# Turning the experts' fetched rows as 16-bit halves instead of 4-byte numbers

## The reference, cut to what matters

```python
x = x + L0_gnn(layernorm(x), ...)      # three graph layers, 50000 edges
x = x + L0_ffn(layernorm(x), ...)      # 8 experts,  256 -> 512 -> 256, gelu
x = x + L1_gnn(layernorm(x), ...)      # graph sum and a GRU cell
x = x + L1_ffn(layernorm(x), ...)      # 16 experts, 256 -> 512 -> 256, relu

# inside a mixture, for every expert e
h   = act(x @ W1[e] + b1[e])           # 512 numbers for each row
y_e = h @ W2[e] + b2[e]                # 256 numbers for each row
y   = y + weight_of_e * y_e            # only where e is one of the row's two best
```

## Time and profile before

| | |
|---|---|
| runs of the kernel before, median (lowest to highest) | 1776.88 us (1776.11 to 1778.33) |
| the profiled execution, its own time | 1773.84 us |
| its span in the trace | 1772.1 us |
| mean granted clock of TensorE | 0.891 of full speed |
| busy: PE, DVE, ACT, POOL | 1473.6, 871.9, 481.6, 336.9 us |
| loops of the first mixture, about | 826 to 1033 us |
| loops of the second mixture, about | 1453 to 1696 us |

### The profile page before, as it was taken

How to read it: one execution, slowest core, us unless ns; L and a number is a source line. 1 busy time by engine, 2 the same in 40 slices (tenths; PEclk the granted TensorE clock), 3 DMA queues, 4 the chain that set the end, 5 groups by cost and what they waited for, 6 DMA issues and landing times. The chain is left out here.

```text
span 1772.1 us, 34488 instructions
## 1 busy us (share of the span) xinstructions
PE 1473.6 (83%) x8498; PEld 1031.8 (58%) x8499; DVE 871.9 (49%) x2496; ACT 481.6 (27%) x1231; POOL 336.9 (19%) x391
## 2 busy tenths in 40 slices
PE   4795989989998999975999956998998649999920
PEld 3674744457443855534898932444665638899820
DVE  6996833323222357774222248312888452222258
ACT  2564400012000311112444433001222414444421
POOL 3000210012000300002554420000000514555420
PEclk9555999999999999986999979998999559999965
DMA  4000321123111422222223257202221334332444
GB/s 122 0 0 12 107 75 47 47 75 119 51 50 47 127 91 83 83 76 85 92 95 127 100 155 234 90 24 74 69 67 42 107 134 155 115 115 92 132 129 129
DMA packets 134622, 158.41 MB, mean 89 GB/s; under 512 B 16929, under 2 KB 119698, under 8 KB 134258
## 3 DMA queue, kind: packets, MB, share of 16 engines
q1 hardware_dynamic: 122642, 125.59, 22.4%
q0 software_dynamic: 11840, 32.12, 6.0%
q10 hardware_dynamic: 96, 0.20, 0.0%
HBM read 103.12 MB, written 57.93 MB: 91 GB/s over the span
## 5 line engine op out<-in xcount | busy, mean ns | idle before, releaser
L875 PE MATMUL agg_ps<-parts,counts 128*128 128x512 f16 x1875 | 410.5, 380 | 8.7 <-PEq L653 8.0
L875 PEld LDWEIGHTS agg_ps<-parts,counts 128*128 (+1 forms) x1875 | 183.6, 98 | 227.6 <-issue 13.5
L1441 ACT ACTIVATE experts_hT<-experts_ps_h,experts_b_col 128x128 f32<-128x128 f32 x456 | 165.8, 367 | 186.4 <-PE experts_ps_h L1416 161.1
L1424 PE MATMUL experts_ps_y<-experts_rows,experts_hT 128*128 128x256 f32 x688 | 163.0, 380 | 0.0
L1379 POOL DMA_INDIRECT chosen<-experts_y,experts_row x116 | 114.6, 988 | 146.6 <-issue 107.9
L1368 POOL DMA_INDIRECT experts_fetched<-tokens,experts_index x120 | 116.1, 967 | 93.9 <-ACT experts_x L1445 41.0
L777 POOL TENSOR_TENSOR parts<-proj_rest,gru_rows 128x256 f32 (+2 forms) x75 | 54.4, 726 | 416.8 <-DVE proj_rest L755 416.8
L1424 PEld LDWEIGHTS experts_ps_y<-experts_rows,experts_hT 128*128 128x128 f32 x688 | 124.3, 191 | 13.4
L1416 PE MATMUL experts_ps_h<-experts_xT,experts_rows 128*128 128x128 f32 x976 | 122.1, 279 | 8.9 <-issue 7.8
L1416 PEld LDWEIGHTS experts_ps_h<-experts_xT,experts_rows 128*128 128x128 f32 x976 | 118.9, 194 | 17.5 <-issue 13.8
L1465 DVE COPY experts_xT<-experts_ps_x 128x256 f32<-128x256 f32 x114 | 48.4, 425 | 162.4 <-PE experts_ps_x L1405 162.4
(11 more groups left out here) (314 smaller groups left out, 2039.5 us busy)
## 6 DMA issues: line engine op xcount, KB each, us to landing
experts_rows<-in_L_ffn_w SPq DMA_DIRECT2D x32, 512.0 KB, 4.8
gru_rows<-x SPq DMA_DIRECT2D x75, 128.0 KB, 2.2
own<-proj_own SPq DMA_DIRECT2D x75, 128.0 KB, 1.7
gru_rows<-own SPq DMA_DIRECT2D x75, 128.0 KB, 2.1
h<-agg_out SPq DMA_DIRECT2D x50, 128.0 KB, 1.7
gru_rows<-h SPq DMA_DIRECT2D x50, 128.0 KB, 2.0
gru_rows<-chosen SPq DMA_DIRECT2D x50, 128.0 KB, 2.3
combine_y<-chosen SPq DMA_DIRECT2D x50, 128.0 KB, 2.1
```

Source lines behind the costliest of these rows:

```text
L875: last = nc.tensor.matmul(ps[b][:], cst.counts[:, s, bass.ds(t * P, P)], parts[:, s, :], start=s == 0, stop=s == NT - 1)
L1424: last = nc.tensor.matmul(ps_y[:, 0:D], hT[:, c, :], down[b][:, c, :], start=c == 0, stop=c == KH - 1)
L1441: nc.scalar.activation(hT[:, c, :], ps_h[c][:, 0:P], function, bias=b1_col[:, bass.ds(e * KH + c, 1)]).then_inc(hT_ready, 1)
```

## The change

The program gets a second identity matrix in 16-bit numbers (`ident16`), which POOL converts from the first in `build_counts`. In `turn`, the tile of 4-byte numbers is viewed as 16-bit numbers, and its lower and its upper halves are turned apart: per half of 128 columns two transposes of 128 by 128 16-bit numbers, four per tile instead of two. The view steps over every second 16-bit number, so the stationary operand is read with a step of 4 bytes. `ps_x` holds 16-bit numbers now, 512 per partition instead of 256. DVE's copy (the new helper `join`) reads them in order and writes each half back beside the other, with a step of 4 bytes, so that `xT` holds 4-byte numbers again. Nothing else in the loop is changed.

```diff
@@ build_counts, GpSimd
                 nc.gpsimd.memset(far_at[:, 0:1], 0.0)
+                nc.gpsimd.tensor_copy(cst.ident16[:], cst.ident[:])
@@ run_experts
-        ps_x, ps_y, ps_b = pb("ps_x", [P, KD, P]), pb("ps_y", [P, BANK]), pb("ps_b", [P, BANK])
+        ps_x = ctx.enter_context(nc.psum_tensor(tag + "ps_x", [P, KD, 2, P], F16))
+        ps_y, ps_b = pb("ps_y", [P, BANK]), pb("ps_b", [P, BANK])
@@ TensorE
                 def turn(q):
                     pe.wait_ge(x_ready, q + 1)
+                    half = x[:].bitcast(F16).rearrange("p (c n h) -> p c h n", c=KD, h=2)
                     for c in range(KD):
-                        last = nc.tensor.transpose(ps_x[:, c, :], x[:, c * P:(c + 1) * P], cst.ident[:])
+                        for h in range(2):
+                            last = nc.tensor.transpose(ps_x[:, c, h, :], half[:, c, h, :], cst.ident16[:])
                     last.then_inc(x_turned, 1)
@@ VectorE
+                def join(ready):
+                    nc.vector.tensor_copy(xT[:].rearrange("p c n -> p (c n)").bitcast(U16).rearrange("p (c n h) -> p c h n", c=KD, h=2),
+                                          ps_x[:].bitcast(U16)).then_inc(ready, 1)
@@ VectorE, before the loop and in it
-                nc.vector.tensor_copy(xT[:], ps_x[:]).then_inc(xT_ready, 1)
+                join(xT_ready)
@@ four_blocks
+        cst.ident16 = sb("ident16", [P, P], F16)
```

More of the change, by code:

```diff
@@ L18 @@
 F16 = mybir.dt.float16
+U16 = mybir.dt.uint16
 I32 = mybir.dt.int32
```

## The result

The change makes the kernel slightly slower: 1782.84 us in the median of 20 runs (1779.36 to 1786.21), against 1779.03 us for the kernel before in 20 runs on the same chips (1774.9 to 1780.62). The ratio is 1.0025, with a 95% interval from 1.0019 to 1.0031, so +4.4 us (3.4 to 5.5). The profiled execution of the change took 1780.89 us, with a span of 1779.1 us. The forecast was 1781.2 us, +4.3, from a before of 1776.88 us.

A forecast was written before the change was run, and what follows sets the result against it. PE's issue was taken to bound both mixture loops. Turns with edges (+0.033 us x 114 = +3.8) and first-tile copies (+0.5) gave +4.3 us on 1776.88, so 1781.2 us, range 1776 to 1809.

The forecast's parts named there:

- The bound: Both mixture loops: time is what PE issues, 3.74 us per tile, 114 tiles.
- The price of four turns: Turn on PE: four 16-bit turns cost 0.223 us per tile where two 4-byte turns cost 0.22.
- The choice of 55.7 ns against 114: One 16-bit turn on PE: strided load stays under the 55.7 ns stream; line 517's strided pair took 114 ns.
- Rival B: Turns on PE: load and stream run one after another, 83.4 ns per turn, 1793.8 us in all; chance 0.15.
- The 27.7 ns: Contiguous 16-bit load of 128 columns on PE, from 25 loads with one-column multiplications; lower bound of one turn.
- The edge: PE passing into 16-bit work and back, once per tile: 0.03 us for both, between 0 and 0.08.
- The prediction's own signs: Turn, period and copy times to check; period growing beyond the turn means unnamed cost, in-loop xT waits a wrong DVE part.
- A: The forecast case: four turns cost what two did, edges aside; 1777 to 1786 us, period 3.74 to 3.78; chance 0.50.
- The copy: DVE's copy to xT grows by 0.27 to 0.69 us, hidden in the loop by PE's second multiplication; price 0.
- The 0.5 us before the two first tiles: Before each mixture's first tile nothing hides the longer DVE copy: 2 x 0.27 = +0.5 us.
- The identity on POOL: One 128 x 128 conversion on POOL, 0.2 to 1 us, ahead of a 125.9 us wait for PE; price 0.
- The sum: Whole kernel: +3.8 us of turns and edges plus +0.5 us of first-tile copies, +4.3 us.

The follow-up runs named there:

- load_step8: The change with the turns' stationary operand read with a step of 8 bytes instead of 4; one execution 1784.63 us against 1775.95 before, tile 3.79 us.
- stream_step8: The change with the 16-bit identity, the moving operand, read with a step of 8 bytes; one execution 1801.83 us against 1775.95 before, tile 3.97 us.
- extra256: The change plus one unused 16-bit multiplication of 256 columns behind the four turns; one execution 1787.51 us against 1773.42 before, median tile period 3.85 us.
- spread_turns: The change with its four turns apart, one at each pair of 4-byte multiplications of the first matrix; one execution 1806.64 us against 1775.95 before, tile 3.95 us.
- copy_alone: The kernel before, its two 4-byte turns kept, with only DVE's copy made as long as in the change (512 2-byte elements); ratio to before 0.9999.
- change_again: The unaltered change timed once more, on one chip; ratio to the kernel before 1.0027, +4.8 us (3.0 to 6.4).
- turns_again: The change with a 256-element copy of upper halves only, no joining, timed again on one chip; ratio to before 1.0016, +2.8 us (0.7 to 5.2).
- turns_alone: The change with a 256-element copy of upper halves only, no joining, first timing, 5 runs; ratio to before 1.0035, +6.2 us (3.9 to 8.5).

## Why the prediction was right, point by point

**The bound.** PE's issue was the bound in both loops, and stayed it: what a tile's work on PE grew by, its period grew by, and 0.3 us more on DVE cost nothing, one tile apart.

**The price of four turns.** 0.223 us was worked out from a 512-column stream, and 0.22 to 0.23 measured. This was the term said to decide, and it was right. The choice of 55.7 ns against 114 for a strided load was right, and load_step8 and stream_step8 show the reason: a step slows the stream and not the load. What the Trainium skill says on this point ("TensorE: Matmul & The Clock Gate", section "Weight-path perf modes — Fast Weight Load (FWL) and DoubleRow"), that the fast load works on strided operands too, the runs bear out as far as a pace can: with steps of 4 and of 8 bytes a turn stays at 56 ns.

**Rival B** falls: loads and streams of short 16-bit pairs overlap. The rule of the Trainium skill of about 81 ns for a pair with 128 columns ("TensorE: Matmul & The Clock Gate", section "Back-to-back issue gap") does not hold here; the four pairs measured 56 ns each. The 27.7 ns that the prediction takes for a bare load was read at 9.23 us, ahead of the first record of the clock in the trace (37.2 us), so the clock it stands for is not known, and no run measured a bare load in the loops.

**The edge.** This is the term that was mis-sized, and its name was wrong. I took 0.03 us, between 0 and 0.08, for going over between types, there and back. Going over to the turns costs nothing: the first multiplication still takes 1.78 us and the four turns 0.22. Coming back costs 0.05 to 0.06 us, and it is no cost of the types: it is the part of the next 4-byte load that a 16-bit turn doesn't cover, 56 ns in the first instruction behind the turns. extra256 makes it vanish with the types unchanged, and spread_turns multiplies it by four. A row of before bounded it: 4-byte multiplications of 128 columns run at 0.112 us, so their loads need no more than that, and at most 0.056 us of one can stay open behind a stream of 0.056. The prediction's own signs showed the miss: the turn came out as A has it, but the period of 3.79 us lies above A's 3.74 to 3.78 and grew by more than the turn, which was to show a cost not named. The Trainium skill ("TensorE: Matmul & The Clock Gate", section "LDWEIGHTS (loading the stationary operand)") gives columns divided by 1.2 for a load in ns, by which an estimate for 128 columns is 107 ns; 107 - 56 = 51 is near the 53 to 56 ns that are left open.

**The copy** was put at 0.69 us and took 0.734; copy_alone shows no price of it in the loop. In the profiled execution of the change it did come on the path once, which was to be a sign that the part on DVE is wrong:

```profile
1683.30 0.39 PE L1410 MATMUL experts_ps_x<-ident,experts_x 128*128 128x128 f16 x4
...
1685.01 0.73 DVE L1458 COPY experts_xT<-experts_ps_x 128x512 uint16<-128x512 uint16 x1 [1.93 <-PE experts_ps_x L1410]
...
1685.79 2.05 PE L1421 MATMUL experts_ps_h<-experts_xT,experts_rows 128*128 128x128 f32 x16 [0.32 <-DVE experts_xT L1458]
```

The copy began 1.71 us after the turns, where it begins 0.43 us after them elsewhere, and 425 ns would have ended 0.31 us sooner. change_again has the same wait in the same tile (0.34 us), while in turns_again, whose short copy begins as late in that tile (1.69 us), PE's multiplications don't wait. So beside late turns the longer copy cost 0.3 us once, and not 0. Why the copy begins late is open.

The 0.5 us before the two first tiles was wrong. From the first turn to the first multiplication it was 1.74 us before:

```profile
824.54 0.69 PE L1405 MATMUL experts_ps_x<-ident,experts_x 128*128 128x128 f32 x2 [3.70 <-DVE experts_x L1455]
...
826.28 3.37 PE L1416 MATMUL experts_ps_h<-experts_xT,gru_rows 128*128 128x128 f32 x16 [1.05 <-DVE experts_xT L1457]
```

and it is 1.74 us after:

```profile
823.86 0.61 PE L1410 MATMUL experts_ps_x<-ident,experts_x 128*128 128x128 f16 x4 [3.85 <-DVE experts_x L1464]
...
825.60 3.78 PE L1421 MATMUL experts_ps_h<-experts_xT,gru_rows 128*128 128x128 f32 x16 [1.13 <-DVE experts_xT L1458]
```

The wait was put down to DVE, but PE started 0.59 us after the copy's end before (825.69) and 0.36 us after it now (825.24); something else ended last, which I take to be PE's own reading of the loop bounds (argued, not tested). The 1.74 us do not change either in extra256, where one more multiplication stands on PE there (826.14 to 827.88). A releaser that is long done when the waiter starts is the sign to look for.

**The identity on POOL** took 491 ns and hid.

**The sum.** 0.06 us x 114 = +6.8 us, of which about 0.5 is the turn's own and the rest the open load. Timed, the kernel lost 4.4 us (3.4 to 5.5). So that the forecast of +4.3 met the time is luck: the edge was too small by 3 us, the 0.5 us for the first tiles did not come, and about 2 us came back that I did not forecast. In the profiled execution the two loops, each taken from the start of its first multiplication to the end of its last, grew from 447.7 to 457.8 us together, by 10.1, 6.8 of it the tiles' period, the rest for the most part single late tiles of the second mixture. The latest, 1.0 us, is in the timeline of the change:

```profile
1463.53 0.98 POOL L1371 DMA_INDIRECT experts_fetched<-tokens,experts_index  x1 [1.41 <-DVE experts_index L1476]
...
1467.31 1.00 POOL L1382 DMA_INDIRECT chosen<-experts_y,experts_row  x1 [2.80 <-DMA chosen<-experts_y,experts_row]
...
1468.73 0.97 POOL L1371 DMA_INDIRECT experts_fetched<-tokens,experts_index  x1 [0.42 <-issue]
...
1473.73 0.99 POOL L1382 DMA_INDIRECT chosen<-experts_y,experts_row  x1 [4.03 <-issue]
...
1473.77 0.40 ACT L1450 COPY experts_x<-experts_fetched 128x256 f32 x1 [3.16 <-POOLq L1367]
...
1474.23 0.40 PE L1410 MATMUL experts_ps_x<-ident,experts_x 128*128 128x128 f16 x4 [0.42 <-ACT experts_x L1450]
```

PE waited for ACT's copy, and ACT for POOL. It was no late fetch: there are two buffers, so this copy takes what was fetched at 1463.53, and that had landed by 1467.84. But POOL reports a fetch only when the next one into the same buffer is due, behind two stores, and it starts the second store (1473.73) only when the first (1467.31) has landed. By the semaphore events of the trace it got past that wait at 1472.69, 5.4 us after the first store began (2.5 us in the median), and reported the fetch at 1473.55. The kernel before has the same order; there the same wait ended 4.1 us after its store, and PE lost nothing. In six tiles, the one at 1683 among them, DVE's copy begins 0.4 to 1.3 us later behind the turns than elsewhere, and in most of them ACT's pieces come late with it; in the trace of before no copy does. These six come to some 2 us, and what delays them is open. At the same time the rest of the program was 3 us shorter than before. Neither was the same in the profiled executions of change_again, turns_alone and turns_again: the loops grew by 11.3, 6.1 and 8.8 us there, and the rest was 1.4, 1.5 and 2.6 us shorter. What gives the 2 us back is left open; a single execution differs from the next by as much.

None of the versions run here beats the kernel before. What would cover the load costs at least as much stream as it saves, as extra256 shows, and the 4-byte turns cover it for nothing.

## What to carry to other kernels

A transpose of 4-byte numbers runs at half the speed of a 16-bit one here, and not at a quarter, so splitting it into halves buys nothing on TensorE: two at 109 ns or four at 56. When a stream of short instructions is put ahead of one with a slower weight load, subtract: what the last short stream doesn't cover of the next load (here 0.05 to 0.06 us) is paid once for each such place, so group the short ones, and don't spread them. Keep the step on the stationary side, where it was free, and off the moving side, where it doubled the time.

## What the runs showed of the hardware that was not expected

- A 16-bit moving operand with a step of 8 bytes streams at 112 ns for 128 columns at a granted clock of 1.00, against 56 ns with adjacent columns. The same step on the stationary operand costs nothing in the pace: the loads' duration rises from 98 to 113 ns, and a turn stays at 56.
- DVE copies 512 2-byte elements from PSUM, written with a step of 4 bytes, in 734 ns. That is 42 ns more than the 692 ns of 512 4-byte elements of another operation with two sources: moving 2 bytes at a time gave no speed in this form.
- The exposed weight load does not appear as a wait or a gap of PE. It is inside the duration of the first multiplication behind it (435 ns for 379).
- POOL reports a fetch that landed at 1467.84 only at 1473.55, because a store of its own had to wait for the landing of the one before. The wait shows on ACT as one for POOL's queue, and not for a DMA: go back through the engine that is named, and look at what it waited for.
